# Who passes on that gathered rows have landed: SyncE once per group of four, instead of GpSimd once per slot

## What is computed

```python
items_emb = item_table[items]
user_emb = user_table[users]
hist_emb = user_table[history_users]                     # 2048 x 100 x 128
scores = jnp.einsum('bhd,bd->bh', hist_emb, user_emb)
user_his_emb = jnp.einsum('bh,bhd->bd', scores, hist_emb)
x = jnp.concatenate([items_emb, user_his_emb, user_emb], axis=1)
x = _dice(_batchnorm(x @ W1 + b1, g1, be1), a1)          # 384 -> 1024
x = _dice(_batchnorm(x @ W2 + b2, g2, be2), a2)          # 1024 -> 512
return x @ W3 + b3
```

## Time and profile before

| what | us |
|---|---|
| timed executions, median of 3 (lowest, highest) | 751.94 (751.31, 752.42) |
| span of the profiled execution, first to last instruction | 998.4 |
| first and last gather of the stream start at, in the profiled execution | 28.5 and 808.4 |
| GpSimd busy in the 432 gathers | 412.1 |

### The profile page before, as it was taken

One profiled execution on the slowest core, in us unless ns is written; L12 is line 12 of the kernel. 1 busy time (PEld: TensorE's weight loads), 2 busy tenths in 40 slices (PEclk: granted clock), 3 DMA queues, 4 the chain that ended last, 5 costly groups with the idle time before them and its releaser, 6 DMA issues.

```text
span 998.4 us, 16415 instructions
## 1 busy us (share of the span) xinstructions
PE 659.4 (66%) x3753; PEld 616.1 (62%) x3753; DVE 523.1 (52%) x1353; ACT 341.5 (34%) x884; POOL 495.0 (50%) x561
## 2 busy tenths in 40 slices
PE   4564665648374655646567556755766479999998
PEld 4463565647364555646466555745665479888877
DVE  7633444335253535444445354554434537999758
ACT  3112222223131322223223222322223248777546
POOL 6646454564646363645554636555554534290036
PEclk8775575757667766667766767768676679999999
DMA  7112111111111111111111111111111110000000
GB/s 214 45 30 45 33 36 33 40 42 30 45 27 43 27 45 30 40 34 35 35 38 33 45 30 40 35 35 40 38 37 33 43 22 2 1 1 1 0 1 2
DMA packets 17237, 34.62 MB, mean 35 GB/s; under 512 B 8104, under 2 KB 8400, under 8 KB 17168
## 3 DMA queue, kind: packets, MB, share of 16 engines
q0 software_dynamic: 14208, 29.13, 11.9%
q1 hardware_dynamic: 2960, 4.67, 1.4%
HBM read 33.76 MB, written 0.01 MB: 34 GB/s over the span
## 4 chain that ended last, share of the span: by engine, by line
PE 46%; another core or an unknown queue 25%; issue 14%; ACT 6%; ACTq 4%; DVE 4%; PEld 0%; DVEq 0%; PEldq 0%
PE ps L1487 15%; PE ps L1546 10%; PE ps L1408 6%; PE ps L1424 4%; ACT scaled L1237 3%; ACTq L1237 2%; PE ps L1474 2%; PE ps L1497 1%; PE ps L1468 1%; PE ps L1561 1%; PE ps L1429 1%; PE ps L1644 1%; PE ps L1457 1%; ACT last_scaled L1247 1%
## 5 line engine op out<-in xcount | busy, mean ns | idle before, releaser
L520 POOL DMA_INDIRECT rows<-in_L_rec_user_table_dram,slot_idx x432 | 412.1, 954 | 374.3 <-ACT scaled L1237 236.6
L1487 PE MATMUL ps<-ident,scaled 128*128 128x128 f32 x984 | 211.6, 384 | 219.9 <-ACT scaled L1237 186.4
L1487 PEld LDWEIGHTS ps<-ident,scaled 128*128 128x128 f32 x984 | 188.8, 285 | 235.4 <-issue 234.5
L1237 ACT ACTIVATE scaled<-rows,work 128x128 f32 (+1 forms) x492 | 157.7, 392 | 253.8 <-remote 168.1
L812 DVE TENSOR_TENSOR prod<-rows,ps 128x512 f32<-128x512 f32 x122 | 83.7, 686 | 156.3 <-POOLq L527 78.3
L1408 PEld LDWEIGHTS ps<-wide,h 128*128 128x128 f32 x512 | 102.5, 299 | 36.5 <-issue 36.5
L1408 PE MATMUL ps<-wide,h 128*128 128x104 f32 x512 | 106.2, 385 | 27.1 <-issue 27.0
L689 DVE SCALAR_TENSOR_TENSOR h<-ps,col_no 128x1024 f32<-128x1024 f32 (+1 forms) x34 | 39.2, 1160 | 154.9 <-ACT ranked L1205 112.0
L1546 PE MATMUL ps<-h,w 128*128 128x256 f32 (+1 forms) x576 | 113.3, 356 | 1.0 <-DVE h L1042 1.0
L1546 PEld LDWEIGHTS ps<-h,w 128*128 128x128 f32 x576 | 99.6, 190 | 12.8 <-issue 1.2
L818 DVE TENSOR_REDUCE work<-prod 128x512 f32 (+1 forms) x122 | 83.7, 686 | 38.2 <-issue 20.5
(11 more groups left out here) (217 smaller groups left out, 805.2 us busy)
## 6 DMA issues: line engine op xcount, KB each, us to landing
rows<-in_L_rec_user_table_dram,slot_idx POOLq DMA_INDIRECT x432
w<-in_L_rec_W_dram SPq DMA_DIRECT2D x1, 2048.0 KB, 18.0
w<-in_L_rec_W_dram SPq DMA_DIRECT2D x1, 1536.0 KB
h<-in_r_history_users_dram SPq DMA_DIRECT2D x2, 400.0 KB, 3.5
wide<-in_L_rec_user_table_dram,own_idx POOLq DMA_INDIRECT x5
wide<-in_L_rec_item_table_dram,own_idx POOLq DMA_INDIRECT x5
last_row<-in_L_rec_user_table_dram SPq DMA_DIRECT2D x1, 64.0 KB
last_item<-in_L_rec_item_table_dram SPq DMA_DIRECT2D x1, 64.0 KB
```

Of the source, the lines that this page charges most:

```text
L520: nc.gpsimd.indirect_dma_start(rows[:, s, :], None, user_table, bass.IndirectOffsetOnAxis(slot_idx[:, s:s + 1], 0)).then_inc(landed[s], 16)
L1237: nc.scalar.activation(scaled[:, j, :], rows[:, bass.ds((g & (GROUPS - 1)) * GROUP + j, 1), :], ACT.Copy, scale=score[:, bass.ds(g * GROUP ...
L1487: mm = nc.tensor.matmul(pooled_ps, scaled[:, j, :], ident[:, :], start=False, stop=False, skip_group_check=True)
```

## The change

`landed` has one semaphore for each of the ring's four groups, in place of one for each of 16 slots; the four gathers of a group all raise the same one, by 64 in a round. GpSimd's `relay` is gone. SyncE has one instead: for group after group it waits until the semaphore stands at 64 times the round, and adds 4 to `arrived` at once. It runs after SyncE's loads and before its wait for the output; the loop's count is read from `ends`, as GpSimd reads its own. What VectorE waits for is written as before.

```diff
-        landed = [sem(f"landed{j}") for j in range(RING)]
+        landed = [sem(f"landed{q}") for q in range(GROUPS)]
...
             sp.dma_start(w2[:, :, :], W2.rearrange("(k p) n -> p k n", p=P)).then_inc(w2_loaded, 16)
+
+            def relay(q, rounds):
+
+                sp.wait_ge(landed[q], rounds * (16 * GROUP))
+                sp.sem_inc(arrived, GROUP)
+
+            for q in range(GROUPS):
+                relay(q, 1)
+            sp.wait_ge(plan_ready, 1)
+            with sp.Fori(1, (end_of(sp, TILES - 1) >> 4) + 1) as r:
+                for q in range(GROUPS):
+                    relay(q, r + 1)
+            sp.sem_inc(stream_over, 1)
             sp.wait_ge(y_kept, 1)
...
-                                             bass.IndirectOffsetOnAxis(slot_idx[:, s:s + 1], 0)).then_inc(landed[s], 16)
-
-            def relay(q, count):
-
-                for j in range(GROUP):
-                    pool.wait_ge(landed[q * GROUP + j], count)
-                    pool.sem_inc(arrived, 1)
+                                             bass.IndirectOffsetOnAxis(slot_idx[:, s:s + 1], 0)).then_inc(landed[q], 16)
...
                     gather(q, j)
-                    if q and j == GROUP - 2:
-                        relay(q - 1, 16)
...
                         gather(q, j)
-                        if j == GROUP - 2:
-                            if q:
-                                relay(q - 1, 16 * r + 16)
-                            else:
-                                relay(GROUPS - 1, 16 * r)
-            relay(GROUPS - 1, 16 * rings)
-            pool.sem_inc(stream_over, 1)
```

## The result

| kernel | timed, us: median (lowest, highest) | ratio, 95% interval |
|---|---|---|
| before | 751.62 (750.77, 752.42) | |
| after | 755.39 (754.74, 755.75) | 1.0046 [1.0032, 1.006] |

A forecast was written before the change was run, and what follows sets the result against it. The prediction took GpSimd's gathering without a pause from 28.5 to 570 us to bound the timed kernel. Its terms, 0 + 0 + 0 + 2.13 us on 751.94, gave 754.1 us, with a range from 750.0 to 756.0.

The forecast's parts named there:

- The profiler's own load: In the stream: GpSimd's 251.7 us standing still and 249.6 us nameless waiting are the profiler's, absent from timed executions.
- The pace sum: Whole span: first gather at 28.5 us, 431 paces of 1.254, then 3.6 and 178.4 us, giving 751.0 us.
- The relay off GpSimd: GpSimd's queue: removing 432 waits and increments gains 0, at most 32.4 us; rival that it held up gathers, chance 0.02.
- SyncE's relay: On SyncE: the moved waits and signals cost 0, with 0.2 us either way.
- Earlier arrival with a full ring: VectorE's group waits: earlier signals gain 0, bound 3.6 us; rival that the ring fills in timed executions, chance 0.12.
- The prediction's own test: Profile after the change: a span more than 10 us below 998.4 would mean VectorE's lateness did matter.
- The argument that VectorE runs ahead of ScalarE: In the stream: ScalarE waits only 3.6 us for VectorE's scores, so SyncE's relay time is hidden outside the last group.
- The last group: Group 107's three end parts all wait for slot 3: 2.13 us slower, bounds 0 to 2.75; rival hidden end, chance 0.34.
- The rule on partial counts: Shared group semaphore: only its full count shows landed data, so the end costs 2.13 us; usable partial counts would give 0.
- TensorE's clock: Start of the second half: a longer lull could leave the first matmuls at a lower clock, up to 3 us, chance 0.06.

The follow-up runs named there:

- part 3: Third batch of follow-up runs, with edits of both kernels and the changed kernel repeated; there the kernel before took 992.1 to 1002.1 us over 29 executions.
- e0: The kernel before, unchanged, profiled a second time; 753.31 us in one execution, span 751.6 us.
- e1: The changed kernel with SyncE relaying each slot by itself, on 16 semaphores; 751.39 us, ratio 0.9992 to the kernel before.
- e4: The kernel before, its GpSimd relay untouched, with all three end parts of the last group waiting for slot 3; 756.78 us, ratio 1.0068.
- e5: The changed kernel with SyncE signalling once per group for three groups of a round, per slot for the fourth, which includes the last group; 750.31 us, ratio 0.9989.
- parts 1 and 2: First two batches of follow-up runs, on the relay and on the last group; the kernel before took 752.50 us in the first and 751.71 us in the second.
- e11: The changed kernel, unchanged, timed again beside the kernel before at 998 us; 984.09 us, ratio 0.9874.
- e6: The changed kernel with the last group weighed in one part of four slots instead of three parts; 754.78 us, ratio 1.0032 to the kernel before.
- e7: The changed kernel with 12 instead of 8 idle products on TensorE before its wait for the last group; 752.89 us, ratio 1.0021 to the kernel before.

## Why the prediction was right, and where its reasons weren't

The time forecast, 754.1 us with a range from 750.0 to 756.0, stands against 755.39 measured. Point by point:

1. **"The profiler's own load": wrong in its cause, right in its use.** 246.5 us were ascribed to the profiler, because three numbers were nearly equal. In every later run the profiled execution took what the others of its kernel took, some at 750 us and some at 990 (its span is 1.7 to 1.8 us shorter than its time), and in part 3 the timed executions of before take 998 us themselves. The surplus is a way in which this kernel runs, profiled or not. What the step was used for held: the timed executions on which the result rests have none of these waits, and e0 shows it (GpSimd's 431 gaps sum to 132.7 us, none over 0.98 us). The timed executions of before, at 752 us, spoke for that regime, but nothing said that the changed kernel's would fall into it too, and that they did is in part luck: in the other one the change gives -1.3%.
2. **The pace sum: right to 0.6 us, by terms that cancel.** 751.0 was forecast for the span's work, e0 spans 751.6. But the first gather starts at 24.2, not 28.5; 431 paces take 543.9 us, not 540.5 (1.262 each; the gap's mean was 0.308, where 0.30 was used); the last multiply comes at +4.03, not +3.61; the rest takes 179.4, not 178.4. And the rest of 0.9 us is the 1.7 us around the span, less the 0.8 by which e0's own time, 753.31, lies over the median of its part.
3. **The relay off GpSimd, taken as 0 (bound 32.4 gain): measured 0.6 to 1.9 us gain, 1.3 us of gaps in the traces.** The reading that its instructions hide behind the gather was right for nearly all groups. The step that failed is that it took a few groups' gaps for all and didn't ask what the queue's lead covers. The two gaps are in the profile of before too (1.09 and 0.96 us), but among 52 longer than 0.35 us.
4. **SyncE's relay, 0 within 0.2 us: right.** A signal takes 17 ns on SyncE too, and e1 is no slower than before. VectorE's waits for the relay didn't shrink at this pace, 112.6 us in e0 and 103.1 after, since what it waits for is the landing itself: the signal comes 2.5 us after the gather's start in the middle.
5. **Earlier arrival with a full ring, 0 (bound 3.6): right for the timed executions, in which the ring never holds GpSimd up; wrong for the other regime.** The bound, what ScalarE lacked of VectorE's scores directly, was passed by far there, with 12.6 us. The prediction's own test, "if the span falls by more than 10 us, VectorE's lateness did matter", was met against the profile that it named, 998.4 to 987.7, and about half of that or more came behind the last gather, where the prediction looked for a loss. The argument that VectorE runs ahead of ScalarE, taken from its 3.6 us, doesn't hold in the timed regime: there ScalarE waits 138 to 140 us for the scores. The term is 0 there for another reason, which is that the landings set the pace.
6. **The last group, 2.13 us (0 to 2.75): the mechanism right, the size 2.56.** The sum had VectorE behind itself in the third part before, at +3.61. In fact the last slot arrives later than the middle one: in the changed kernel the signal came at +3.49, where 2.5 is the middle. In e0 the old third part starts at +4.03, 0.74 us after VectorE was free for it, behind its landing, and the three parts behind one signal cost nearly the whole upper bound of 1.51 + 1.24. e4 and e5 show the mechanism: the common wait alone brings the cost, the parts' own signals take it away. The rule on partial counts (the Trainium skill, page "DMA: Bandwidth & Descriptors", section "Why a DMA increments its semaphore by 16 and not by 1") wasn't tested, since no run here reads a partial count; e1 and e5 give the parts their own slots by separate semaphores, and get the cost back.
7. **TensorE's clock: underrated.** Put at a chance of 0.06 and up to 3 us on top, it came in the profiled execution of the changed kernel with 1.5 us, and the medians with and without more idle products differ by 1.9 us. The prediction named the place and the price but read no granted clock there, neither in the stretch before the last group nor in the matmuls after it; the chance had no row under it.

The sum put together afterwards: 2.56 (parts) + 1.5 to 1.9 (clock) - 0.8 to 1.3 (GpSimd's relay, by e5 and by e0's gaps) = 2.8 to 3.7 us, against 3.5 measured. The forecast of 2.1 missed two terms of opposite sign, and that they nearly cancel is luck. The mechanism that it was built on, the last group's parts waiting together, is the one that the runs show.

## What to carry to other kernels

A signal that gathers several landings costs nothing where the consumer waits for all of them anyway. It costs where the consumer works piece by piece and the end of the program hangs on it: the work on the earlier pieces then no longer runs while the last one is landing. Keep the fine signal for the last group, and the coarse one elsewhere (e5). Taking waits off an engine that feeds a stream may be worth something even where its gaps look untouched, because its queue then runs further ahead and covers pauses. Before a large difference between profiled and timed executions is ascribed to the profiler, profile again.

## What was not expected of the hardware

**Two regimes of one program.** The kernel before took 750.5 to 753.6 us in parts 1 and 2, and 992 to 1002 in part 3; parts 1 and 3 ran on one and the same chip, so the chip isn't what differs. What the slow one looks like can be read: TensorE's signals come late while GpSimd gathers. In e11, ScalarE waits with its next scaling for the signal of a matmul group of TensorE (eight matmuls from 295.43, over at 296.49) until 304.37, two us after GpSimd has run out of free slots:

```profile
295.43 1.06 PE L1485 MATMUL ps<-ident,scaled 128*128 128x128 f32 x8
...
301.39 0.94 POOL L533 DMA_INDIRECT rows<-in_L_rec_user_table_dram,slot_idx  x1 [0.30 <-issue]
304.37 1.28 ACT L1235 ACTIVATE scaled<-rows,work 128x128 f32 x4 [8.94 <-remote]
...
306.45 0.94 POOL L533 DMA_INDIRECT rows<-in_L_rec_user_table_dram,slot_idx  x1 [4.12 <-ACT scaled L1235]
```

Counted over the trace, 120 of TensorE's signals reach their semaphore over 1.5 us after the matmul's end in the profile of before (724 us in sum), 111 in e11 (657 us), one in the changed kernel's and none in e0. Some updates are missing from these records (119 of 124 of one of TensorE's semaphores are there in before), so a few of the 120 may be gaps in the record. Of the 120, 94 come in a pause of GpSimd of over 1 us, in the middle 1.8 us after its last gather has ended; of the 111, 96. Then ScalarE is late, the ring fills, GpSimd stops, the signals come, and it starts over. That is the order of things in the traces; why a signal waits for GpSimd's pause, and what puts a run into this regime, is open.

**The last landing is slow.** From a gather's start to SyncE's signal it takes 2.5 us in the middle (2.4 to 4.2 in e1), but for the last gather 3.5 to 3.8 us in each of after, e1, e5, e6, e7 and e11. In e1 the four of the last group take 2.5, 2.7, 3.1 and 3.7 us. Why is open.
